# Attention plus top-2 experts on one core: experts read their weights in place, the bias comes from ScalarE, the dispatched rows are fp32

## The chip, the cores and the metric

The kernel is one launch on one NeuronCore of a Trainium2 chip. It is timed in device microseconds, as the median of several executions. Engines are named as in the profile: PE (TensorE, with PEld for its weight loads), DVE (VectorE), ACT (ScalarE), POOL (GpSimd) and SP (the queue that issues most transfers).

## The reference, cut to what matters

```python
xn = layernorm(x)                      # x is (2, 1024, 128)
# attention, causal, one head of 128
k, q, v = xn @ Wk.T + bk, xn @ Wq.T + bq, xn @ Wv.T + bv
attn = softmax(where(causal, q @ k.T * 128 ** -0.5, -inf)) @ v
# experts: 16, of which each token takes 2; hidden size 512
logits = xn @ Wr + br
topv, topi = top_k(softmax(logits), 2)
h = relu(xn @ W1[e] + b1[e])           # for both experts of the token
y = h @ W2[e] + b2[e]
out = x + attn + sum over the two experts of gate * y
```

There are 2048 tokens, so 16 tiles of 128 tokens, 16 experts, and 4096 pairs of token and expert.

## The kernel before

The program is written by hand for each engine; an engine runs its list in the order in which it stands, and semaphores join the lists. Five stages follow each other, with work of the next stage put into gaps of the one before.

1. **Front.** x comes in four groups of four tiles. DVE takes the moments (L641, L644), ACT the root (L498), DVE normalises into `xn` (L651). PE transposes (L903), ACT copies to `xT` (L503), PE multiplies with the router weights (L909). Before its first transpose of x, PE waits in its list for the loads of Wq, Wk, Wv, bq and bk (`proj_in`) and transposes the three matrices (L920).
2. **Routing.** When all logits are there, DVE chooses the two best experts of each token with compares and maxima over 128x256 (L703 to L719). PE counts ranks (L954 to L958) and DVE turns them into one slot number for each pair (L727 to L746). Between these, PE projects q, k and v (L942, L946) and ACT copies them out of PSUM (L534, L537).
3. **Dispatch and attention, tiles 0 to 12.** POOL scatters the normalised rows, 32 times 128 rows, into a table in DRAM of 47 tiles of 128 slots, sorted by expert (L467). A row is the fp16 high half, the fp16 low half, the number of the pair and the gate. The table was filled first with one blank row everywhere (L339). Beside this, PE, DVE and ACT do the attention: scores (L974), row maximum (L763), exponential (L558), transposes (L987), copies (L567, L773), product with v (L1005), sum into x (L783). Into this loop ACT's squares of the weights (L524) and fp16 high parts (L548), DVE's low parts (L755) and four of POOL's six high parts (L447) are put. Each expert's W1 and W2 are scaled by a power of two and kept as high and low fp16 halves; the fp32 weights come through a ring of six places (`raw`).
4. **Experts, 47 tiles.** Each tile belongs to one expert, whose number the engines read at run time. For each tile SP copies the expert's "kit" (W2 in two halves, a selector row, b2, a factor: 352 KB) from one place of SBUF to another (L351). PE transposes the slot rows (L1038, L1039), ACT copies them (L596), PE adds b1 with four matmuls against the selector (L1074) and multiplies with W1, three fp16 matmuls for each of four chunks (L1080, L1081, L1083). ACT takes the relu (L613), DVE the low half (L855), PE multiplies with W2, twelve matmuls (L1051 to L1053), DVE scales and adds b2 (L845), ACT multiplies with the gate (L602), POOL scatters the result rows by pair number (L478).
5. **Tail.** Attention of the three last tiles, then the two expert rows of each token are added to x by DVE (L871) and POOL (L487), and stored (L386).

PE runs two tiles deep: the W2 product of tile j-2 is laid between the chunks of tile j, and the transposes of tile j+2 follow. The address of each W1 chunk is worked out on PE's sequencer from the expert's number. The number is loaded once a tile:

```python
if c == 1 and j + 1 < TILES:
    after = expert_of(j + 1)        # one value_load a tile
if r is not None:
    if c == 1:
        result_waits(r); result(r, 0); result(r, 1)
    elif c > 1:
        last = result(r, c)
```

Of the kernel before, what the change touches and what calls it, by code (L numbers as in the profile page):

```python
# [11 lines left out]
I32 = mybir.dt.int32  # L12

P = 128
# [3 lines left out]
def attention_and_top2_experts(nc, x, Wk, bk, Wq, bq, Wv, bv, Wr, br, W1, b1, W2, b2, out):  # L18

# [12 lines left out]
    assert D == P and HID == NCH * P  # L36


    ROW = 2 * D + 4

    W1_HI, W1_LO, KIT_AT = 0, HID, 2 * HID
    W2_HI, W2_LO, SEL, B2F = 0, HID, 2 * HID, (2 * HID + P) // 2
    CF = B2F + D
    KIT = 2 * (CF + 1)
    EW = KIT_AT + KIT
    RAW = 6
    WG = 2
    NST, NHB, NYB = 7, 3, 6  # L50
    XG = [0, 6, 16, 32, TILES]
    WL = [*range(0, E - 1, 2), E - 1, E]
# [3 lines left out]
    LATE = 3  # L56

    slots_dram = nc.dram_tensor("slots_dram", (P * TILES, ROW // 2), I32).ap()
    pairs_dram = nc.dram_tensor("pairs_dram", (NT * P * K, D), F32).ap()

    with ExitStack() as ctx:
# [6 lines left out]

        xin = sb("xin", [P, NT, D], F32)
        xn = sb("xn", [P, NT, D], F32)  # L70
# [4 lines left out]
        wts = sb("wts", [P, E, EW], F16)  # L75
        raw = sb("raw", [P, RAW, 2, HID], F32)
        probsT0 = sb("probsT0", [P, 2, G * P], F32)
# [3 lines left out]
        b1rows = sb("b1rows", [P, HID], F32)  # L81

        b1parts = [sb(f"b1parts{n}", [P, HID], F16) for n in range(2)]
        mv = sb("mv", [P, NT, 2], F32)
        std = sb("std", [P, NT], F32)
        rstd = sb("rstd", [P, NT], F32)
        epsc = sb("epsc", [P, 1], F32)
        ident = sb("ident", [P, P], F32)
        ident16 = sb("ident16", [P, P], F16)

# [3 lines left out]
        scratch_i = sb("scratch_i", [P, 1], I32)  # L94
        past = sb("past", [P, E], F32)
        best = sb("best", [P, K, NT], F32)
        pick = sb("pick", [P, NT], F32)
        gap = sb("gap", [P, NT], F32)
        slotrow = sb("slotrow", [P, K, NT], I32)
        cnt = sb("cnt", [P, E], I32)  # L100
        ntile = sb("ntile", [P, E], I32)
        ntilef = sb("ntilef", [P, E], F32)
        cum = sb("cum", [P, E], F32)
        start = sb("start", [P, E], F32)
        expertf = sb("expertf", [P, 1], F32)
        expert = sb("expert", [P, 1], I32)
# [6 lines left out]
        b1s = sb("b1s", [P, 1], F32)  # L113
        b1tmp = sb("b1tmp", [P, E], F32)
        diag = sb("diag", [P, E], F32)
# [5 lines left out]

        slot_space = sb("slot_space", [P, TILES * ROW], F16)
        slots = slot_space[:, :].rearrange("p (t c) -> p t c", t=TILES)
# [9 lines left out]
        def early(n, parts=P):  # L133
            a = 2 * taken[0]
            taken[0] += n
            assert 2 * taken[0] <= stage_w + ybuf_w
            return space[0:parts, a:a + 2 * n].bitcast(F32)
# [1000 lines left out]
```

## Time and profile before

| | us |
|---|---|
| median of 3 executions | 242.03 |
| lowest, highest | 241.85, 243.75 |
| span of the profiled execution, first to last instruction | 237.6 |
| from the span to the median | 4.4 |

| stage | us from the span's start |
|---|---|
| first PE work on the loaded matrices | 8.5 |
| slot numbers of all pairs ready, first row maximum | 43.8, 43.9 |
| first matmul of the first expert tile | 111.9 |
| last W2 matmul of the last expert tile | 214.9 |
| end | 237.6 |

The profiled execution has no time of its own here beside its span. Busy time is 174.0 us on PE, 135.2 on DVE, 119.0 on ACT and 121.4 on POOL, so that no engine is busy throughout, and the stages have to be read one by one. In the page's slices PE is busy for a tenth or less from about 75 to 90 us, in the middle of the attention.

### The profile page before, as it was taken

What the parts mean: (1) busy time and instruction counts of PE and PEld (TensorE: products, weight loads), DVE (VectorE), ACT (ScalarE), POOL (GpSimd) and SP (SyncE); (2) the same over time, 40 slices, a digit from 0 to 9 for tenths busy, and PEclk for the clock granted to TensorE, in tenths of its full rate; (3) what the DMA queues carried; (4) which work ended last, traced back from release to release, by engine and by line L of the source; (5) the groups of instructions that cost most, each with busy time, mean ns of one, the idle gap of its engine ahead of it and who ended that gap; (6) DMA issues with size and microseconds to landing.
All of it is one profiled execution on the core that took longest, in us unless ns stands there. A gap on an engine that the chain in (4) does not pass through costs nothing.

```text
span 237.6 us, 5504 instructions
## 1 busy us (share of the span) xinstructions
PE 174.0 (73%) x1852; PEld 147.5 (62%) x1852; DVE 135.2 (57%) x318; ACT 119.0 (50%) x262; POOL 121.4 (51%) x146
## 2 busy tenths in 40 slices
PE   7549969759675002995989788988989879968940
PEld 7449645438474001874888777877878769855740
DVE  3893789798531004579768945444444543445491
ACT  1425496767541004496859546455464564544500
POOL 8593906388777770015049864534535445346250
PEclk9995597997958755599999999999999999999996
DMA  5879999419966110524995364653655554300682
GB/s 156 238 259 257 165 141 149 126 37 335 289 212 262 45 56 11 177 80 168 316 360 217 145 244 146 228 187 150 234 183 198 207 212 159 139 25 0 191 274 66
DMA packets 30202, 41.82 MB, mean 176 GB/s; under 512 B 5665, under 2 KB 18347, under 8 KB 29920
## 3 DMA queue, kind: packets, MB, share of 16 engines
q1 hardware_dynamic: 27648, 37.24, 52.6%
q0 software_dynamic: 2528, 4.24, 5.4%
q8 instruction: 16, 0.26, 0.5%
q14 instruction: 10, 0.08, 0.1%
HBM read 16.09 MB, written 9.39 MB: 107 GB/s over the span
## 4 chain that ended last, share of the span: by engine, by line
PE 37%; DVE 26%; another core or an unknown queue 17%; issue 10%; ACT 7%; DMA 1%; DVEq 0%; ACTq 0%
PE pO L1051 4%; DVE wts L755 4%; PE pS L1083 4%; DVE xn L651 4%; PE pS L1074 4%; PE pO L1005 4%; PE pS L974 3%; PE pS L1080 3%; PE pS L1081 3%; ACT xT L596 3%; PE pO L1053 2%; PE pO L1052 2%; PE pT L1039 2%; PE pT L987 2%
## 5 line engine op out<-in xcount | busy, mean ns | idle before, releaser
L478 POOL DMA_INDIRECT pairs_dram<-space,slot_space x47 | 48.8, 1038 | 56.4 <-ACT space L602 47.8
L855 DVE SCALAR_TENSOR_TENSOR xT<-pS,xT 128x512 f16<-128x512 f32 x47 | 32.5, 691 | 45.3 <-issue 22.9
L1051 PE MATMUL pO<-space,xT 128*128 128x128 f16 x188 | 38.5, 219 | 10.6 <-issue 6.0
L613 ACT ACTIVATE xT<-pS 128x512 f16<-128x512 f32 x47 | 27.9, 594 | 32.0 <-PE pS L1083 26.4
L467 POOL DMA_INDIRECT slots_dram<-slot_space,slotrow x32 | 34.6, 1080 | 14.8 <-issue 9.5
L1080 PE MATMUL pS<-xT,wts 128*128 128x128 f16 x188 | 38.8, 219 | 0.3 <-issue 0.3
L1083 PE MATMUL pS<-xT,wts 128*128 128x128 f16 x188 | 38.8, 219 | 0.0
L1081 PE MATMUL pS<-xT,wts 128*128 128x128 f16 x188 | 38.8, 219 | 0.0
L1052 PE MATMUL pO<-space,xT 128*128 128x128 f16 x188 | 38.5, 218 | 0.0
L1053 PE MATMUL pO<-space,xT 128*128 128x128 f16 x188 | 38.5, 218 | 0.0
L1051 PEld LDWEIGHTS pO<-space,xT 128*128 128x128 f16 x188 | 18.2, 97 | 15.0 <-issue 9.6
L987 PE MATMUL pT<-ident,xn 128*128 128x128 f32 x72 | 12.3, 302 | 20.3 <-ACT xn L558 20.2
L987 PEld LDWEIGHTS pT<-ident,xn 128*128 128x128 f32 x72 | 9.3, 156 | 24.3 <-ACT xn L558 23.6
L447 POOL TENSOR_TENSOR wts<-raw,wscale 128x1024 f16<-128x1024 f32 x6 | 11.4, 1906 | 23.7 <-DVE wscale L672 23.7
L755 DVE SCALAR_TENSOR_TENSOR wts<-raw,wscale,wts 128x1024 f16<-128x1024 f32 x16 | 23.2, 1450 | 0.2 <-ACT wts L548 0.2
L596 ACT COPY xT<-pT 128x256 f16<-128x256 f16 x47 | 17.4, 372 | 11.0 <-remote 7.6
L1074 PE MATMUL pS<-space,b1parts 128*128 128x128 f16 x188 | 18.6, 221 | 4.4 <-ACT xT L596 2.7
L1081 PEld LDWEIGHTS pS<-xT,wts 128*128 (+1 forms) x188 | 21.5, 115 | 0.5 <-issue 0.4
L1080 PEld LDWEIGHTS pS<-xT,wts 128*128 (+1 forms) x188 | 21.5, 114 | 0.3
L1083 PEld LDWEIGHTS pS<-xT,wts 128*128 (+1 forms) x188 | 21.5, 115 | 0.0
L974 PE MATMUL pS<-kT,qT 128*128 128x512 f32 (+3 forms) x48 | 20.1, 539 | 0.7 <-ACT v L537 0.7
L602 ACT ACTIVATE space<-space,slot_space 128x128 f32<-128x128 f32 x47 | 19.2, 411 | 2.3 <-DVE space L845 2.3
(144 smaller groups left out, 396.1 us busy)
## 6 DMA issues: line engine op xcount, KB each, us to landing
space<-wts SPq DMA_DIRECT2D x47, 352.5 KB
raw<-in_L_ffn_W SPq DMA_DIRECT2D x14, 512.0 KB, 5.3
slots_dram<-space SPq DMA_DIRECT2D x1, 3055.0 KB, 27.4
raw<-pairs_dram SPq DMA_DIRECT2D x8, 256.0 KB, 5.0
slot_space<-slots_dram SPq DMA_DIRECT2D x1, 1040.0 KB, 8.8
xin<-in_L_attn_x SPq DMA_DIRECT2D x4, 256.0 KB, 3.5
wts<-in_L_ffn_b SPq DMA_DIRECT2D x1, 1024.0 KB, 29.7
raw<-in_L_ffn_W SPq DMA_DIRECT2D x4, 256.0 KB, 2.9
```

The source lines that it names most:

```text
L467: pool.indirect_dma_start(slots_dram, bass.IndirectOffsetOnAxis(ap=slotrow[:, k, t:t + 1], axis=0), rows_i[:, k, t, :], None).then_inc(row ...
L478: pool.indirect_dma_start(pairs_dram, bass.IndirectOffsetOnAxis(ap=slots_i[:, j, D:D + 1], axis=0), ybuf[:, j % NYB, :], None, bounds_chec ...
L613: nc.scalar.activation(hid[:, j % NHB, 0, :], pA(j), ACT.Relu).then_inc(hi_done, 1)
L755: dve.scalar_tensor_tensor(out=low_part(e), in0=raw[:, e % RAW, :, :], scalar=wscale[:, e:e + 1], in1=high_part(e), op0=ALU.mult, op1=ALU. ...
L855: dve.scalar_tensor_tensor(out=hid[:, j % NHB, 1, :], in0=pA(j), scalar=0.0, in1=hid[:, j % NHB, 0, :], op0=ALU.max, op1=ALU.subtract).the ...
L1051: pe.matmul(y, h_hi, w_hi, start=(c == 0), stop=False)
L1052: pe.matmul(y, h_hi, w_lo, start=False, stop=False)
L1053: return pe.matmul(y, h_lo, w_hi, start=False, stop=(c == NCH - 1))
L1074: pe.matmul(bank[:, c * P:(c + 1) * P], b1parts[j >= B1_SECOND][:, c:HID:NCH], stage[:, j % NST, SEL:SEL + P], start=(c == 0), stop=False, ...
L1080: pe.matmul(to, w_hi, x_hi, start=False, stop=False, skip_group_check=True)
L1081: pe.matmul(to, w_hi, x_lo, start=False, stop=False, skip_group_check=True)
L1083: ins = pe.matmul(to, w_lo, x_hi, start=False, stop=(c == NCH - 1), skip_group_check=True)
```

## The change

- **Front.** ACT normalises (with a bias that DVE prepares), directly into fp32 rows of 128 values plus two numbers. DVE chooses the two best experts by `max` and `max_index`, one group of four tiles at a time, between the moments of later groups. The blank table is filled right after the loads of x, before the loads of Wq, Wk, Wv, bq and bk, in pieces of four rows (2,080 B) instead of one (520 B).
- **Weights.** `wts` has 18 places of 4 KB for each partition; the fp32 weights of expert e come into place e+2, all of them at once, and the fp16 halves are written into places e and e+2, in place. The ring, the kits and their copies, the selector and `b1rows` are gone. b2 stands in a table of its own. ACT makes all high parts, POOL none.
- **Attention.** Tiles 0 to 13 stand before the experts, 14 and 15 behind. The v bias is added by DVE when it copies v out of PSUM. The rank comes from a running sum of the choices and only the counts go through PE.
- **Experts.** ACT writes b1 of the tile's expert into the PSUM bank before the matmuls, which add to it. The slot rows are transposed once in fp32; ACT writes the high half, DVE the low half. The numbers of the experts are loaded in batches of twelve. W1 and W2 are both read from `wts` at an address worked out from the number. W1's twelve matmuls and W2's twelve stand one after the other. The gate isn't in the slot row: the final sum multiplies with it.
- **Tail.** DVE makes the final sum alone, 32 operations of 128x128, once all attention tiles are done.

Cut to its core:

```diff
-    ROW = 2 * D + 4
-    RAW = 6
-    NST, NHB, NYB = 7, 3, 6
-    XG = [0, 6, 16, 32, TILES]
-    LATE = 3
+    ROW = D + 2
+    NHB, NYB, NXS, NPB = 3, 6, 3, 4
+    XG = [0, 4, 12, 24, TILES]
+    IDS = 12
+    LATE = 2
+    NBL = 4
 # SP
             load_x(3)
+            sp.wait_ge(blank_made, 1)
+            sp.dma_start(blank_v[:, 0:whole, :].rearrange("p (m n) c -> p m (n c)", n=NBL),
+                         blank_i.rearrange("p n c -> p (n c)")[:, None, :].broadcast_to([P, TILES // NBL, NBL * ROW])
+                         ).then_inc(blank_sent, 16)
+            sp.dma_start(blank_v[:, whole:TILES, :], blank_i[:, 0:TILES - whole, :]).then_inc(blank_sent, 16)
             for n, w in enumerate((Wq, Wk, Wv)):
                 sp.dma_start(wqkv[:, n, :], w).then_inc(proj_in, 16)
...
-            sp.dma_start(slots_v, blank[:, None, :].broadcast_to([P, TILES, ROW // 2])).then_inc(blank_sent, 16)
...
+            for n in range(1, NW):
+                load_weights(n)
 # ACT
+            def normalise(g):
+                act.wait_ge(nbias_done, g + 1)
+                for t in range(G * g, G * g + G):
+                    ins = nc.scalar.activation(rows[:, t, 0:D], xin[:, t, :], ACT.Identity, bias=nbias[:, t:t + 1],
+                                               scale=rstd[:, t:t + 1])
+                ins.then_inc(xn_done, 1)
             for g in range(NG):
                 std_of(g)
+                normalise(g)
                 if g == 0:
                     act.wait_ge(wT_done, 1)
...
+            def put_bias(j):
+                load_ids(j)
+                ...
+                nc.scalar.copy(pA(j).rearrange("p (c s) -> p c s", s=P),
+                               b1s[:, bass.ds(ids[j], 1), :].rearrange("p a c -> p (a c)")[:, :, None].broadcast_to(
+                                   [P, NCH, P])).then_inc(bias_put, 1)
 # DVE
+            def choose(g):
+                dve.wait_ge(logits_done, g + 1)
+                ...
+                for t in tiles:
+                    ins = dve.max(top[:, t, :], lg[:, t, :])
+                step(ins)
+                for t in tiles:
+                    ins = dve.max_index(pick[:, t, :], top[:, t, :], lg[:, t, :])
+            moments(0)
+            moments(1)
+            inverse_std(0)
+            moments(2)
+            inverse_std(1)
+            dve.wait_ge(router_in, 32)
+            dve.wait_ge(consts, 1)
+            choose(0)
+            moments(3)
+            inverse_std(2)
+            choose(1)
+            inverse_std(3)
+            choose(2)
+            step(choose(3))
...
             def combine(n):
                 dve.wait_ge(pairs_in[n], 16)
                 for k in range(K):
-                    ins = dve.tensor_tensor(xin[:, here, :], xin[:, here, :], pairs[:, here, k, :], ALU.add)
+                    for t in range(TYL * n, TYL * n + TYL):
+                        ins = dve.scalar_tensor_tensor(out=xin[:, t, :], in0=pairs[:, t, k, :],
+                                                       scalar=gate[:, k, t:t + 1], in1=xin[:, t, :], op0=ALU.mult,
+                                                       op1=ALU.add)
 # PE
+            router(NG - 1)
+            for n in range(4):
+                project_qk(n)
+            pe.wait_ge(sofar_done, 1)
...
+            def hidden(j):
+                load_ids(j)
+                e = ids[j]
+                pe.wait_ge(bias_put, j + 1)
+                pe.wait_ge(xs_lo, j + 1)
+                pe.wait_ge(wlo_done, min(j, E - 1) + 1)
+                for c in range(NCH):
+                    w_hi = part(e, HI)[:, :, c:HID:NCH].rearrange("p a h -> p (a h)")
+                    w_lo = part(e, LO)[:, :, c:HID:NCH].rearrange("p a h -> p (a h)")
+                    pe.matmul(to, w_hi, x_hi, start=False, stop=False, skip_group_check=True)
+                    pe.matmul(to, w_hi, x_lo, start=False, stop=False, skip_group_check=True)
+                    ins = pe.matmul(to, w_lo, x_hi, start=False, stop=True, skip_group_check=True)
```

In the fences below, `ISA` is a register instruction of PE's sequencer that works out an address from the expert's number, and the rows are in the order of PE's list. One expert tile before, from the first W1 chunk of a tile in mid-stage to the third (L1080 to L1083 are W1, L1051 to L1053 are W2):

```order
L1080 ISA
L1080 MATMUL pS<-xT,wts 128x128
L1081 MATMUL pS<-xT,wts 128x128
L1083 ISA
L1083 MATMUL pS<-xT,wts 128x128
L1051 MATMUL pO<-space,xT 128x128
L1052 MATMUL pO<-space,xT 128x128
L1053 MATMUL pO<-space,xT 128x128
```

The same place now, at the change from W1 (L981 to L983) to W2 (L999 to L1001):

```order
L981 ISA
L981 MATMUL pS<-xT,wts 128x128
L982 MATMUL pS<-xT,wts 128x128
L983 ISA
L983 MATMUL pS<-xT,wts 128x128
L999 ISA [waits y_done,lo_done]
L999 MATMUL pO<-wts,xT 128x128
L1000 ISA
L1000 MATMUL pO<-wts,xT 128x128
L1001 MATMUL pO<-wts,xT 128x128
```

The W2 matmuls had none of these rows and now have two for each three matmuls, as W1 has: 16 a tile instead of 8.

SP's list before, from the last load of x:

```order
L309 DMA xin<-in_L_attn_x 128x4x128
L318 DMA space<-in_L_attn_Wq 128x128
L318 DMA space<-in_L_attn_Wk 128x128
L318 DMA space<-in_L_attn_Wv 128x128
L319 DMA bqk<-in_L_attn_bq 128x1
L320 DMA bqk<-in_L_attn_bk 128x1
```

And now:

```order
L287 DMA xin<-in_L_attn_x 128x4x128
L303 DMA slots_dram<-slots 128x11x520 [waits blank_made]
L306 DMA slots_dram<-slots 128x390
L308 DMA slots<-in_L_attn_Wq 128x128
L308 DMA slots<-in_L_attn_Wk 128x128
L308 DMA slots<-in_L_attn_Wv 128x128
L309 DMA bqk<-in_L_attn_bq 128x1
L310 DMA bqk<-in_L_attn_bk 128x1
```

The fill of the table, 3 MB, moved from behind three pairs of weight loads to ahead of the five loads that PE's first work waits for.

## Rows read from the trace of the kernel before

**Rows 1.** The page's first line, and what the DMA engines moved in 40 equal slices.
```profile
span 237.6 us, 5504 instructions
...
GB/s 156 238 259 257 165 141 149 126 37 335 289 212 262 45 56 11 177 80 168 316 360 217 145 244 146 228 187 150 234 183 198 207 212 159 139 25 0 191 274 66
```
**Rows 2.** The fill's transfer: count, KB each, median us from issue to landing.
```profile
slots_dram<-space SPq DMA_DIRECT2D x1, 3055.0 KB, 27.4
```
**Rows 3.** Order of time, front: start, us, engine, line, operation, count, [idle before <-releaser].
```profile
8.53 0.55 PE L920 MATMUL pO<-ident,space 128*128 128x128 f32 x3 [2.10 <-DMA bqk<-in_L_attn_bk]
19.16 1.73 PE L909 MATMUL pO<-wr,xT 128*128 128x16 f32 x8
20.73 1.09 PE L903 MATMUL pT<-ident,xn 128*128 128x128 f32 x4
24.89 3.76 PE L942 MATMUL pS<-xT,space 128*128 128x512 f32 x4
43.92 0.29 DVE L763 CUSTOM_DVE_ANT_0 pS<-pS,causal 128x128 f32<-128x128 f32 x1
```
**Rows 4.** Groups by line: count, busy us, mean ns | idle before, its releasers.
```profile
L602 ACT ACTIVATE space<-space,slot_space 128x128 f32<-128x128 f32 x47 | 19.2, 411 | 2.3 <-DVE space L845 2.3
L641 DVE BATCH_NORM_STATS2 space<-xin 128x6 f32<-128x128 f32 x16 | 3.4, 276 | 3.8 <-DMA xin<-in_L_attn_x 3.8
L534 ACT ACTIVATE kT<-pS,bqk 128x512 f32<-128x512 f32 x4 | 2.7, 687 | 2.0 <-PE pS L942 2.0
L524 ACT ACTIVATE wts<-raw 128x1024 f16<-128x1024 f32 x16 | 17.0, 1063 | 0.2 <-issue 0.2
L543 ACT ACT_TABLE_LOAD x1 | 1.3, 1283 | 0.0
L548 ACT ACTIVATE wts<-raw,wscale 128x1024 f16<-128x1024 f32 x10 | 11.5, 1150 | 5.6 <-DVE wscale L672 5.5 <-issue 0.2
L558 ACT ACTIVATE xn<-pS,negm 128x128 f32<-128x128 f32 (+7 forms) x16 | 12.0, 747 | 5.3 <-DVE negm L763 3.6 <-issue 1.6
L558 ACT ACTIVATION_READ_ACCUMULATOR xn<-pS,negm 128x1 f32 x16 | 3.2, 201 | 0.0
L567 ACT COPY probsT<-pT 128x512 f32<-128x512 f32 (+2 forms) x8 | 3.8, 479 | 5.1 <-remote 2.8 <-PE pT L987 2.3
```
**Rows 5.** Order of time around the idle stretch of the attention: POOL, PE, ACT.
```profile
44.88 1.18 POOL L467 DMA_INDIRECT slots_dram<-slot_space,slotrow  x1 [5.32 <-DVE slotrow L746]
72.73 1.61 PE L1005 MATMUL pO<-v,probsT 128*128 128x128 f32 x12
87.94 0.96 POOL L467 DMA_INDIRECT slots_dram<-slot_space,slotrow  x1 [0.30 <-issue]
92.55 0.59 ACT L567 COPY xT<-pT 128x512 f32<-128x512 f32 x1 [18.96 <-remote]
```
**Rows 6.** Busy time of the expert stage: stretch, length, engines, clock, DMA.
```profile
112.00:215.00 103.00, 88.65 (x1411) 81.21 (x1411) 55.96 (x110) 58.57 (x147) 49.51 (x46) 1.00 0.53 195
```
**Rows 7.** Order of time on PE, second expert tile, full clock.
```profile
113.38 0.22 PE L1080 MATMUL pS<-xT,wts 128*128 128x128 f16 x1
113.43 0.22 PE L1081 MATMUL pS<-xT,wts 128*128 128x128 f16 x1
...
113.68 0.24 PE L1080 MATMUL pS<-xT,wts 128*128 128x128 f16 x1
...
113.93 0.24 PE L1080 MATMUL pS<-xT,wts 128*128 128x128 f16 x1
```
**Rows 8.** Groups by line: the expert tile on ACT and DVE, the final sum.
```profile
L613 ACT ACTIVATE xT<-pS 128x512 f16<-128x512 f32 x47 | 27.9, 594 | 32.0 <-PE pS L1083 26.4 <-remote 4.8 <-issue 0.8
L855 DVE SCALAR_TENSOR_TENSOR xT<-pS,xT 128x512 f16<-128x512 f32 x47 | 32.5, 691 | 45.3 <-issue 22.9 <-ACT xT L613 22.2
L783 DVE SCALAR_TENSOR_TENSOR xin<-pO,rinv,xin 128x128 f32<-128x128 f32 x16 | 5.3, 337 | 2.1 <-issue 2.0
L871 DVE TENSOR_TENSOR xin<-xin,raw 128x256 f32<-128x256 f32 x10 | 5.9, 600 | 2.1 <-DMA raw<-pairs_dram 1.9
```

More of the change, by code:

```diff
@@ L12 @@
 I32 = mybir.dt.int32
+U32 = mybir.dt.uint32
 P = 128
@@ L413, in _ @@
-            step(pool.memset(ones[:, :], 1.0))
-            pool.affine_select(out=later[:, :], in_=later[:, :], compare_op=ALU.is_gt, fill=-1.0,
+            pool.memset(ones16[:, :], 1.0 / P)
+            step(pool.memset(before[:, :], 1.0))
+            pool.affine_select(out=before[:, :], in_=before[:, :], compare_op=ALU.is_gt, fill=0.0,
                                base=0, pattern=[[1, P]], channel_multiplier=-1)
-            for k in range(K):
-                pool.iota(rows_i[:, k, :, D:D + 1], pattern=[[K * P, NT], [0, 1]], base=k, channel_multiplier=K)
@@ new lines, in _, with scales @@
+            dve.wait_ge(ex_done, 1)
+            step(dve.tensor_reduce(exsum[:, :], ex[:, :, :], AX.X, ALU.add))
+            step(dve.reciprocal(gate[:, 0, :], exsum[:, :]))
+            dve.tensor_tensor(gate[:, 1, :], gate[:, 0, :], gap[:, :], ALU.mult).then_inc(gates_done, 1)
+            def scales(g, bank):
+                s = slice(WG * g, WG * g + WG)
+                dve.wait_ge(sums_done, g + 1)
+                step(dve.tensor_scalar(expo[:, s], bank[:, s].bitcast(I32), 1, None, ALU.logical_shift_right))
@@ new lines, in _, with load_ids @@
+            dve.wait_ge(cf_made, 1)
+            dve.tensor_copy(cf[:, :], pO[1][:, 0:TILE_COLS]).then_inc(cf_done, 1)
+            ids = {}
+            def load_ids(j):
+                if j % IDS == 0:
+                    z = min(j + IDS, TILES)
+                    _, got = nc.values_load_multi_w_load_instructions(
+                        erow[0:1, j:z], engines=[mybir.EngineType.DVE], min_val=0, max_val=E - 1,
+                        skip_runtime_bounds_check_because="the numbers of experts are clamped")
+                    ids.update(zip(range(j, z), got))
@@ new lines, in _ @@
+            pe.wait_ge(sofar_done, 1)
+            count = sofar[:, :, NT - 1]
+            pe.matmul(pO[0][:, 0:E], before[:, :], count, start=True, stop=True)
+            pe.matmul(pO[0][:, E:2 * E], ones16[:, :], count, start=True, stop=True).then_inc(ranks_done, 1)
+            for n in range(4, 2 * NG):
+                project_qk(n)
+            for g in range(NG):
+                project_v(g)
+                if g == 0:
+                    pe.wait_ge(consts, 2)
+                    pe.wait_ge(spread_done, 1)
+                    pe.matmul(pO[1][:, 0:TILE_COLS], ones[:, :], spread[:, :], start=True, stop=True).then_inc(erow_made, 1)
```

900 lines of the change are left out of this document (378 added, 522 removed).

## The prediction

> **What bounds the kernel now.** I read the page first for the span and the slices, then the order of time stage by stage, then the groups by line for durations. The profiled execution spans 237.6 us [rows 1]; the median of the runs is 242.03, so 4.4 us lie around the span, and I add them at the end.
>
> Four stages follow each other. The front ends with the first row maximum, at 43.9 [rows 3]. The attention and the weights last until the experts begin, 68.0 us later, at 111.9 (table of stages). In the middle of them is a hold: PE runs its product with v at 72.7, but ACT's next copy starts only at 92.55, after 19.0 us of idle time that no signal of this trace closes ("remote"); POOL's scatters run from 44.9 to 88.9, and the copy comes 3.6 us after the last [rows 5]. That the scatters delay PE's signals is my reading of this neighbourhood, not something that a row states. The experts take 103.0 us for 47 tiles, 2.19 each, with PE busy for 88.7 of them at full clock [rows 6]. The tail takes 22.6.
>
> No engine is full throughout, so each stage is costed apart, by the wait that ends last in it.
>
> **The front: later by 17.6 us.** PE's first three transposes start at 8.53, when the last of the five matrix loads is there [rows 3]. Now the fill stands ahead of these loads on the same queue. It moves 3.1 MB; before, behind other loads, it took 27.4 us [rows 2]. How long it takes in 2,080 B pieces no row shows. Bounds: at the fastest slice of the page, 360 GB/s, 8.7 us; at the old time 27.4. I take the slices of the front, about 258 GB/s [rows 1], which gives 12.1, since those slices move similar loads; PE then begins at 20.6 instead of 8.5.
>
> The Trainium skill, "SBUF — State Buffer", section "Summary: rules for kernel authors", says to reckon about 358 GB/s between HBM and SBUF. By that rule the fill would take 8.7 us and the sum would be 3.4 lower. The busiest slice of the trace, 360 GB/s, is at that figure, the slices of the front are well under it.
>
> From there it is one chain, because ACT waits for PE's transposed matrices in its list between the first and the second group's normalising:
> - matrices transposed 0.55, copied out 0.5, root 0.3, DVE's reciprocal and bias 0.5, four normalises at 0.411 (the same shape on ACT, [rows 4]) 1.6, transposes 1.1 and router 1.7 at the lower clock (1.09 and 1.73, [rows 3]): first logits at 26.9.
> - A round for each later group, as choice and bias stand in one list on DVE: choice 2.1, bias 0.4, normalise 1.6, copy 0.6, transposes 1.1, router 1.7 = 7.5. The choice of a group is eight small operations and eight of one tile; I take 2.1 from the small operations of the trace (about 0.15 to 0.3 each). The first round has the last group's moments in it too, four at 0.276 [rows 4] plus as much as one more, 1.3: 8.8. So logits 2 to 4 are complete at 35.7, 43.2 and 45. Two more choices: 47.4.
> - PE projects q and k of half the groups before the ranks, four groups of matmuls, 3.76 at the lower clock [rows 3]: ranks at about 49, slot numbers about 4 later, at 53.
> - ACT meanwhile: the last of eight copies of q and k (0.687, [rows 4]) about 53.7, four squares at 1.06 and their reads to 58.3, table load and exponentials 1.9 (load 1.28) to 60.2; DVE then makes the gates, 1.1, and starts the first row maximum at about 61.5 instead of 43.9: **+17.6**. If the fill is at its bounds, +14.2 or +32.9.
>
> What stands on DVE behind the slots (expert numbers 1.2, four v copies, b1 sums) fits before the gates and costs nothing, unless ACT is earlier than this; then up to 3 us of it show.
>
> **Attention and weights: shorter by 14 us.** POOL's six high parts, the ring and its waits are gone, all weights are loaded ahead. ACT has now the most work: 12 squares at 1.06 (12.7), 13 high parts at 1.15 (15.0), 14 exponentials at 0.747 and a read of 0.201 (13.3), and 14 copies at 0.479 (6.7) [rows 4]: 47.7. With a few per cent for handing over, 50.5, and 3.5 for the last weight half, bias and rows of the first tile, 54 against 68.0: **-14.0**. This counts the hold as gone. Of the 68.0 it was some 20; the new work on ACT gives back 6. The bounds: the whole hold comes back (rival B), or DVE and ACT overlap perfectly, -18.
>
> **Experts: longer by 5.8 us.** Removed: four b1 matmuls, which run at the pitch of 0.055 that three matmuls in a row show [rows 7], 0.2 a tile; the gate operation, 0.411 on ACT, hidden; the kits, off the path. Added: eight address instructions on PE's sequencer for each tile, as W2 is now addressed like W1, and a batch of numbers every twelve tiles instead of one each tile. A W1 group of three matmuls with two such instructions starts 0.25 after the one before it (113.68 to 113.93), though its matmuls need 0.17 [rows 7]. Before, each such group was followed by a W2 group without any, in whose time the sequencer caught up. Now eight groups in a row at 0.25 make 2.0, and the waits and two transposes 0.25: 2.25 a tile. 47 x 2.25 + 3 to fill and drain = 108.8 against 103.0: **+5.8**. ACT would need 0.6 for the bias, 0.594 for the relu and 0.3 for the rows, 1.5; DVE 0.691, 0.3 and 0.34, 1.35 [rows 8]: both fit beside it. Bounds: ACT's work with its waits, 1.75 (rival C); upwards 2.4, if the waits on three semaphores cost twice as much.
>
> **Tail: shorter by 0.6 us.** Two attention tiles instead of three, about 4 us less. The final sum is 32 operations of the kind that takes 0.337, about 10 us with little of POOL's help; before, ten of 0.600 on DVE and six on POOL [rows 8]: +4 on DVE, of which 0.6 fit under the loads. Bounds ±4.
>
> **Sum.** 237.6 + 17.6 - 14.0 + 5.8 - 0.6 = 246.4 span; with 4.4 around it, 250.8, so 251 against 242.03.
>
> **Rivals.**
> - **B, the hold comes back.** The scatters start now at about 54 and take 44 us again (32 at 1.27 and 0.96 to 1.38 each); until 97 they lie beside the attention, which starts at 61.5. For it: the late copies lie within 4 us of the last scatter [rows 5]. If PE's signals are late until some 3.6 us after the last scatter, the attention stands for 10 to 30 us: 261 to 281, about 270. Against it: no kit, no ring and larger pieces stand in the DMA queues now.
>  The Trainium skill, "SBUF — State Buffer", section "SBUF: two separate sides", has it that "A DMA cannot be slowed by a compute op, and vice versa". By that rule alone there would be no hold and B would fall out. The trace speaks against leaning on it: ACT's 19 us idle stand exactly beside POOL's scatters.
> - **C, faster than before: the addresses don't limit.** The queue that fed 113.38 to 113.49 at 0.055 shows that instructions can be ready ahead. If the sequencer works ahead during each tile's waits, the 26 matmuls need 1.45 and ACT or the hand-over sets about 1.75 a tile: 47 x 1.75 + 3 = 85.3, that is -17.7 instead of +5.8, so 251 - 23.5 = 227.5. It decides from about 2.05 a tile on: below it, the kernel is as fast as before or faster. Against it: in steady state nothing replenishes a queue that drains at 0.25 a group.
> - **D, the fill does not hold the loads back.** The fill writes DRAM and the five loads are small; if they land at about 8.5 to 10 all the same, the front is 11 shorter: 240, no change.
> - **Combinations** of B with C, about 246, and of C with D, about 217.
>
> **Chances.** A (251, within 245 to 258) 0.38; B 0.26; C 0.16; D 0.08; B with C 0.06; the rest 0.06. The forecast is A's, 251; its own range 245 to 258. The range to hold 8 in 10 reaches to C's 226 and into B, 274. Faster by over 1% (below 239.6): C, C with D and a third of D, 0.21. Within 1%, which is about what a measurement of this kernel can tell from no change (239.6 to 244.4): the rest of D and the edges, 0.08. Slower by over 1%: A, B and most of B with C, 0.71.
>
> **What would show each step.** PE's first work on the loaded matrices at about 20.6 (17 to 36); were it at 9, D holds. First logits near 27, rounds of 7 to 9. Slot numbers near 53, the first row maximum near 61.5. From there to the first W1 matmul 54 us without a stretch in which PE, DVE and ACT all stand; a stretch of over 5 us beside the scatters is B. ACT's relu in the experts every 2.25 us; under 2.05 is C. The last part after the experts 22 us. The prediction is wrong if the front's loss is off by more than half, or if the expert tile does not keep to the address instructions.

## The result, and the profile after

The changed kernel took 288.12 us (median of 4 runs, 285.85 to 290.4) where the kernel before took 241.94: a ratio of 1.185, interval 1.175 to 1.196. Ratios and intervals are formed from the fast executions alone, those within 1.5 per cent of the fastest of their kernel. The forecast, 251, missed it, and so did its range, 226 to 274.

In the later runs both kernels were faster: before about 210.5 (on four chips), the changed kernel 254.5 (on two of them); ratio 1.210, interval 1.204 to 1.216. The record does not say on which chip the first runs were. The two numbers of the first runs are to be compared with each other, and the later ones with each other. By stage, from one profiled execution of each, in us:

| stage | before, first runs | changed, first runs | before, later | changed, later |
|---|---|---|---|---|
| to the first row maximum | 43.9 | 60.3 | 43.5 | 60.1 |
| to the first W1 or b1 matmul | 68.0 | 86.5 | 52.7 | 55.2 |
| to the first relu | 1.1 | 1.5 | 1.9 | 1.2 |
| relu 1 to relu 47 (46 tiles) | 99.5 | 108.0 | 84.1 | 108.0 |
| to the end | 25.0 | 28.1 | 25.9 | 28.2 |
| span | 237.6 | 284.4 | 208.1 | 252.6 |

The front of the changed kernel, first runs, in order of time: start, duration, and in brackets the idle time before and what ended it.

```profile
20.10 0.90 PE L829 MATMUL pS<-ident,slots 128*128 128x128 f32 x3 [12.31 <-DMA bqk<-in_L_attn_bk]
32.54 1.73 PE L807 MATMUL pO<-wr,xT 128*128 128x16 f32 x8
39.67 3.43 PE L807 MATMUL pO<-wr,xT 128*128 128x16 f32 x16
60.26 0.29 DVE L664 CUSTOM_DVE_ANT_0 pS<-pS,causal 128x128 f32<-128x128 f32 x1
```

PE's first work on the matrices moved from 8.53 [rows 3] to 20.10; the router's rounds start 7 to 8 us apart behind it (the first, left out here, at 25.0), and the first row maximum is at 60.26 (61.5 forecast). The fill itself:

```profile
slots_dram<-slots SPq DMA_DIRECT2D x1, 2860.0 KB, 14.4
```

The attention, first runs, in order of time, PE, ACT and the last scatter:

```profile
61.32 1.21 PE L874 MATMUL pS<-kT,qT 128*128 128x384 f32 x2
...
72.78 0.42 PE L874 MATMUL pS<-kT,qT 128*128 128x128 f32 x1
...
84.59 0.48 ACT L457 COPY probsT<-pT 128x384 f32<-128x384 f32 x1 [13.44 <-remote]
...
86.72 2.54 PE L874 MATMUL pS<-kT,qT 128*128 128x512 f32 x4
...
92.11 0.96 POOL L375 DMA_INDIRECT slots_dram<-rows,slotrow  x1 [0.30 <-issue]
...
98.07 0.59 ACT L457 COPY probsT<-pT 128x512 f32<-128x512 f32 x1 [10.25 <-remote]
...
100.05 0.58 PE L860 MATMUL pO<-sumsq,ones 128*128 128x2 f32 x2 [10.79 <-DVE xin L683]
```

And two of its groups by line:

```profile
L457 ACT COPY probsT<-pT 128x512 f32<-128x512 f32 (+3 forms) x16 | 8.0, 499 | 33.4 <-remote 31.0 <-PE pT L889 2.4
...
L646 DVE TENSOR_SCALAR expo<-pO 128x2 int32<-128x2 int32 x8 | 1.3, 160 | 28.0 <-remote 22.4 <-PE pO L861 5.5
```

The hold of [rows 5] is there again, and longer: ACT waits 31.0 us in all for PE's transposes in waits that the profile puts down to nobody ("remote"), and things move again at 98, some 5 us after the last scatter's end at 93.1. The trace also records when each semaphore rises, and this shows what is late. The semaphore for which the copy at 84.59 waits rose at 84.57, 13.5 us after the transposes that raise it had ended; for the copy at 98.07 it was 11.1 us. In this trace 24 of PE's 222 recorded signals rose over 0.3 us after the end of their instruction, in that of the kernel before 71 of 211, while none of ACT's or DVE's was over 0.03 late. In the 16 later traces none of PE's was over 0.015 late. Ends of matmuls are modelled, so it stays unsaid whether the signal or the end of the matmul itself was late. The same stretch in a later run, same kernel:

```profile
60.29 0.96 POOL L375 DMA_INDIRECT slots_dram<-rows,slotrow  x1 [0.30 <-issue]
...
60.99 0.48 PE L889 MATMUL pT<-ident,probs 128*128 128x128 f32 x1 [2.29 <-ACT probs L448]
...
61.50 0.27 ACT L457 COPY probsT<-pT 128x128 f32<-128x128 f32 x1
61.55 0.96 POOL L375 DMA_INDIRECT slots_dram<-rows,slotrow  x1 [0.31 <-issue]
```

```profile
L457 ACT COPY probsT<-pT 128x512 f32<-128x512 f32 (+3 forms) x16 | 7.9, 496 | 3.5 <-PE pT L889 3.5
```

Here the copy starts 0.03 us after the transpose ends, with the scatters at the same pace beside it, and its group idles 3.5 us instead of 33.4.

In the experts, one tile of the changed kernel, PE in order of time (first runs):

```profile
190.40 0.24 PE L981 MATMUL pS<-xT,wts 128*128 128x128 f16 x1
190.48 0.22 PE L982 MATMUL pS<-xT,wts 128*128 128x128 f16 x1
190.53 0.23 PE L983 MATMUL pS<-xT,wts 128*128 128x128 f16 x1
190.65 0.24 PE L981 MATMUL pS<-xT,wts 128*128 128x128 f16 x1
...
191.57 0.23 PE L999 MATMUL pO<-wts,xT 128*128 x1
191.69 0.23 PE L1000 MATMUL pO<-wts,xT 128*128 x1
191.75 0.22 PE L1001 MATMUL pO<-wts,xT 128*128 x1
191.81 0.23 PE L999 MATMUL pO<-wts,xT 128*128 x1
```

Most groups of three start 0.25 after the one before, W1 and W2 alike, as the groups in [rows 7] did; in this tile it is 0.24 to 0.31, and 0.36 at the change from W1 to W2. Three matmuls need 0.17. Overlapping matmuls count as busy, so the busy time hides these gaps. The tail's final sum is one block of 32 operations:

```profile
272.64 9.49 DVE L773 SCALAR_TENSOR_TENSOR xin<-slots,gate,xin 128x128 f32<-128x128 f32 x32
```

### The profile page after: what moved, and what is told of

Read it like the earlier page. It is cut to its first block, busy times and chain, and to the rows that moved or that the text cites. A ratio compares the mean times of both kernels' runs of the same rounds, so it can differ in the third digit from the quotient of the medians.

```text
span 284.4 us, 5460 instructions
## 1 busy us (share of the span) xinstructions
PE 203.9 (72%) x1628; PEld 161.6 (57%) x1628; DVE 138.8 (49%) x462; ACT 134.3 (47%) x274; POOL 82.0 (29%) x102
## 4 chain that ended last, share of the span: by engine, by line
PE 60%; another core or an unknown queue 11%; DVE 10%; ACT 7%; issue 5%; SPq 4%; DMA 3%; DVEq 0%; ACTq 0%
PE pS L981 8%; PE pO L1000 8%; PE pO L999 7%; PE pS L983 5%; PE pS L874 5%; PE pO L909 4%; PE pS L982 4%; PE pO L1001 4%; PE pS L815 3%; DVE xin L773 3%; PE pT L889 3%; DMA bqk<-in_L_attn_bk 3%; PE pT L966 2%; PE pO L807 2%
## 5 line engine op out<-in xcount | busy, mean ns | idle before, releaser
L382 POOL DMA_INDIRECT pairs_dram<-ybuf,pair x47 | 46.8, 996 | 122.4 <-DVE ybuf L743 116.4
L981 PE MATMUL pS<-xT,wts 128*128 128x128 f16 x188 | 46.8, 249 | 5.1 <-DVE xT L735 3.7
L375 POOL DMA_INDIRECT slots_dram<-rows,slotrow x32 | 31.0, 967 | 56.7 <-DVE slotrow L608 47.2
L983 PE MATMUL pS<-xT,wts 128*128 128x128 f16 x188 | 44.6, 238 | 0.0
L1000 PE MATMUL pO<-wts,xT 128*128 x188 | 42.9, 229 | 0.1
L999 PE MATMUL pO<-wts,xT 128*128 x188 | 42.9, 229 | 0.0
L982 PE MATMUL pS<-xT,wts 128*128 128x128 f16 x188 | 42.4, 226 | 0.0
L1001 PE MATMUL pO<-wts,xT 128*128 x188 | 41.4, 221 | 0.0
L511 ACT ACTIVATE xT<-pS 128x512 f16<-128x512 f32 x47 | 28.1, 597 | 16.2 <-PE pS L983 15.7
L493 ACT COPY pS<-b1s 128x512 f32 x47 | 27.8, 594 | 7.3 <-PE pS L938 4.8
L981 PEld LDWEIGHTS pS<-xT,wts 128*128 x188 | 21.6, 115 | 10.8 <-issue 6.1
L501 ACT CAST xT<-pT 128x128 f16<-128x128 f32 x47 | 12.4, 266 | 28.2 <-PE pT L966 26.6
L889 PE MATMUL pT<-ident,probs 128*128 128x128 f32 x72 | 13.5, 325 | 16.9 <-ACT probs L448 6.9
L982 PEld LDWEIGHTS pS<-xT,wts 128*128 x188 | 25.0, 133 | 0.1
L457 ACT COPY probsT<-pT 128x512 f32<-128x512 f32 (+3 forms) x16 | 8.0, 499 | 33.4 <-remote 31.0
L999 PEld LDWEIGHTS pO<-wts,xT 128*128 128x128 f16 x188 | 18.2, 97 | 7.9
L909 PE MATMUL pO<-v,probsT 128*128 128x128 f32 x144 | 21.9, 306 | 0.0
L983 PEld LDWEIGHTS pS<-xT,wts 128*128 x188 | 21.6, 115 | 0.4
L909 PEld LDWEIGHTS pO<-v,probsT 128*128 128x128 f32 x144 | 20.6, 220 | 1.7 <-issue 1.3
L1000 PEld LDWEIGHTS pO<-wts,xT 128*128 128x128 f16 x188 | 18.1, 96 | 5.9 <-issue 0.2
## 6 DMA issues: line engine op xcount, KB each, us to landing
slots_dram<-slots SPq DMA_DIRECT2D x1, 2860.0 KB, 14.4
```

The lines of the kernel that those rows point to most:

```text
L375: pool.indirect_dma_start(slots_dram, bass.IndirectOffsetOnAxis(ap=slotrow[:, k, t:t + 1], axis=0), rows_i[:, t, :], None).then_inc(rows_s ...
L382: pool.indirect_dma_start(pairs_dram, bass.IndirectOffsetOnAxis(ap=pair[:, j:j + 1], axis=0), ybuf[:, j % NYB, :], None, bounds_check=NT * ...
L511: nc.scalar.activation(hid[:, j % NHB, 0, :], pA(j), ACT.Relu).then_inc(hi_done, 1)
L909: ins = pe.matmul(pO[t % 2][:, 0:D], probsT[t % 2][:, j // G, j % G * P:(j % G + 1) * P], v[:, t // TB * TB + j, :], start=(j == 0), stop= ...
L981: pe.matmul(to, w_hi, x_hi, start=False, stop=False, skip_group_check=True)
L982: pe.matmul(to, w_hi, x_lo, start=False, stop=False, skip_group_check=True)
```

## The experiments

In all of them the kernel before ran beside on the same chip and took 209.7 to 210.5 us.

**1. The fill behind the five loads.** Edit, in SP's list of the changed kernel:

```diff
-            sp.wait_ge(blank_made, 1)
-            sp.dma_start(blank_v[:, 0:whole, :]...)
             for n, w in enumerate((Wq, Wk, Wv)):
                 sp.dma_start(wqkv[:, n, :], w).then_inc(proj_in, 16)
...
+            sp.wait_ge(blank_made, 1)
+            sp.dma_start(blank_v[:, 0:whole, :]...)
```

> The changed kernel with the fill of the slot table moved behind the loads of Wq, Wk, Wv, bq and bk; nothing else. Theory: the 11.6 us by which PE's first work on the matrices came later (20.1 against 8.5) are the fill's, and the front is one chain behind it: PE's three transposes at about 9, slot numbers about 41 instead of 52.2, first row maximum about 49 instead of 60.3. The stretch in which PE's signals come late is tied to the scatters and moves with them, so the total is about 11 us shorter, 275 to 279. Rival: the chain behind is set by other loads (the weights for the squares, the fill for the scatters), and less than 5 us are gained.

Measured: 240.74, span 239.0 against 252.6, so 13.6 less than in a later run of the unchanged kernel.

```profile
8.17 0.55 PE L829 MATMUL pS<-ident,slots 128*128 128x128 f32 x3
...
47.53 0.29 DVE L664 CUSTOM_DVE_ANT_0 pS<-pS,causal 128x128 f32<-128x128 f32 x1
```

PE begins at 8.17 and the first row maximum is at 47.53 instead of 60.09. The expectation had the gain about right (11); its total of 275 to 279 was that of the first runs, with their hold. So 12.6 of the 16.6 us of the front are the fill's place in SP's list. The other 4.0 stay with the new routing and normalising; they were not taken apart.

**2. Two scatters under way at most.**

```diff
+                    pool.wait_ge(rows_sent[i % 2], 16 * (i // 2))
                     pool.indirect_dma_start(slots_dram, ...).then_inc(rows_sent[i % 2], 16)
```

> The changed kernel, but each of the 32 row scatters first waits until the scatter two before it has landed, so that two are under way at most; same work. Theory: PE's signals come late because scatters follow each other every 1.27 us without a pause and their writes pile up; spread to 2 us or more each, the signals are prompt (under 0.5 us), the stretch of 61.6 to 98 is gone, the attention takes about 52 us (60 to 112), and the total falls by 20 to 35 us, to 253 to 268. Rival 1: any scatter beside PE delays it, as many as there are: the delay lasts as long as the scatters do, now longer, and the total is the same or more. Rival 2: the idle stretch is PE's low clock and has nothing to do with POOL: nothing changes.

Measured: 254.64, and 255.22 on another chip. Neither showed late signals, with or without the edit (the unchanged kernel: 254.5), so this tells nothing about them. Nor did the edit pace much: the scatters take 54.5 to 99.5 instead of 52.5 to 95.6, but the usual distance of two of them is 1.27 to 1.28 us, where it is 1.26 without the edit. Even where signals are late it would not have been a clean test of the pace.

**3. The scatters after the attention.**

```diff
                 for t in range(NT):
+                    if k == 0 and t == 2:
+                        pool.wait_ge(o_read, NT - LATE)
```

> The changed kernel, but 30 of the 32 row scatters wait until the attention of tiles 0 to 13 is over. Theory (scatters delay PE's signals): the attention runs without the idle stretch, 60 to about 113, then 30 scatters stand alone, 38 us, and the experts begin at about 113 + 38 + 11 = 162; total about 300. It tells how long the attention is by itself. Rival (the stretch has another cause, the clock or the loads): the attention still takes about 80 us, the experts begin at 190, total near 325.

Measured: 292.37. From the first row maximum to ACT's first bias copy the attention takes 50.9 us (62.1 to 113.0) without scatters, and 52.7 (60.1 to 112.8) with them in a later run of the unchanged kernel; in the other later traces of this attention with scatters it takes 51.2 (experiment 2) to 53.2. So without late signals the scatters cost it 0.3 to 2.3 us in all. Total and stage are near the expectation, but since the unchanged kernel has no hold there either, the two theories were not told apart.

**4. Plain writes of the same rows.** As 3, with this in SP's list:

```diff
+            for i in range(K * NT):
+                sp.dma_start(spare[P * i:P * i + P, :], rows_i[:, i % NT, :]).then_inc(spare_sent, 16)
```

> As the run before (30 of 32 scatters after the attention), and in the time of the scatters SP issues 32 plain transfers of the same rows, 128 pieces of 520 bytes each, to a spare table in DRAM. Theory A: it is POOL's own issuing of descriptors that delays PE: no idle stretch here, attention about 53 us. Theory B: it is the traffic of small writes: the idle stretch is back, attention 70 us or more.

Measured: 291.75, no hold; the attention takes 50.9, as in 3. Inconclusive for the same reason. SP issued the transfers from 54.6 to 68.9, so they lay beside the first part of the attention alone.

**5. Both kernels again, unchanged.**

> The kernel before, unchanged. In the last runs it took 210.5 us beside the experiments, against 241.9 in the runs shown first, and the profile of one experiment showed prompt PE signals beside scatters that follow each other every 1.27 us. Theory: the stretch in which PE's signals come late belongs to the chip or its condition, not to the program: where the total is 210 the stretch 62.5 to 92.5 is gone and the experts are shorter too; where it is 242 it is there. Rival: the two totals differ by something else, such as the clock or the expert stage alone, and the stretch is there in both.

> The changed kernel, unchanged, several rounds beside the kernel before on one chip. Theory: without the late signals, before is 210.5 and the changed kernel 288 less its own stretch (36 us), 250 to 254; the ratio is then near 1.20, made by the front (16 us), the longer expert tile and the handing over. With the late signals, 242 and 288 as before. Rival: the late signals cost both kernels the same, and the difference stays 46 us.

> The changed kernel, unchanged, beside these. 288 where the kernel before takes 242, 254 where it takes 210; a third pairing (288 beside 210, or 254 beside 242) would show that the late signals do not belong to the chip but come and go by the execution.

Measured: before 209.96; changed 254.54 (4 runs; 253.34 to 255.03) and, on a further chip, 254.47. The totals 242 and 288 were seen in the first runs alone, in all 4 executions of each kernel; 210 and 254.5 in all later ones. The same groups of copies in the kernel before, first runs and then a later one:

```profile
L567 ACT COPY xT<-pT 128x512 f32<-128x512 f32 (+1 forms) x8 | 4.2, 528 | 22.1 <-remote 19.0 <-PE pT L987 3.1
L773 DVE COPY xT<-pT 128x256 f32<-128x256 f32 (+1 forms) x4 | 2.2, 555 | 20.5 <-remote 19.9 <-issue 0.6
...
L567 ACT COPY xT<-pT 128x512 f32<-128x512 f32 (+1 forms) x8 | 4.2, 525 | 2.7 <-PE pT L987 2.7
L773 DVE COPY xT<-pT 128x256 f32<-128x256 f32 (+1 forms) x4 | 2.2, 550 | 2.8 <-PE pT L987 2.8
```

So the hold was in the profile from which the forecast was made. By these differences late signals cost the kernel before 15.3 us in the attention (68.0 against 52.7) and as many in the experts (99.5 against 84.1), and the changed kernel 31.3 in the attention and none in the experts.

Why the experts differ can be read from the traces of the first runs. In the kernel before 61 of 134 PE signals of that stage are over 0.3 us late (2.2 at most), and 59 of the 61 lie beside two scatters of result rows that POOL issued back to back; there are 22 such pairs. In the changed kernel there are 6 pairs, and all of its 12 late signals lie beside them. Scatters in pairs are not enough for it, though: the later traces have 4 and 5 pairs and no late signal. The difference of the two kernels is nearly the same with late signals (46.2) and without (44.0), by chance of these sums.

**6. W2 at a fixed place.** Every tile multiplies with expert 0's W2; the result is that of other weights, the work is the same.

```diff
             def result(r):
-                e = ids[r]
+                e = 0
```

> The changed kernel, but the W2 product of every tile reads expert 0's halves at a fixed place: 8 address instructions a tile on PE's sequencer instead of 16, all matmuls kept (the result of the experts is thereby not the reference's). Theory: the tile of 2.35 us is set by the address instructions; 8 fewer at 0.125 give at least 0.5 us back, after which ACT's and DVE's hand-over sets it, 1.75 to 1.85 a tile; relu 1 to relu 47 takes 80 to 86 us instead of 108, total 227 to 232 beside a kernel before of 210. Rival: ACT's three operations and waits, or the order of the matmuls, set the tile: no change, 252 to 255.

Measured: 220.7, 33.8 less than 254.5; 1.65 us a tile on average, 1.51 in the median tile.

**7. W1 fixed as well.** The same edit in `hidden`.

> As the run before, and W1 fixed at expert 0 too: no address instruction for PE is left in the expert tile (the result of the experts is thereby not the reference's). Theory: if the run with W2 fixed was already set by ACT and DVE, this gives little more, 1.7 to 1.85 a tile; if the address instructions still set it, 26 matmuls at 0.055 and the waits remain, 1.5 to 1.6.

Measured: 215.87, 1.55 a tile on average, 1.46 in the median tile. PE's matmuls now start 0.05 to 0.06 apart:

```profile
149.99 0.22 PE L981 MATMUL pS<-xT,wts 128*128 128x128 f16 x1
150.05 0.22 PE L982 MATMUL pS<-xT,wts 128*128 128x128 f16 x1
150.11 0.22 PE L983 MATMUL pS<-xT,wts 128*128 128x128 f16 x1
150.16 0.22 PE L981 MATMUL pS<-xT,wts 128*128 128x128 f16 x1
```

With 16, 8 and 0 address instructions the median tile takes 2.29, 1.51 and 1.46 in the later runs. The first eight cost nearly nothing, the second eight 0.8. The reading that fits all three is that the sequencer has room for eight beside the matmuls and then becomes the bound, at 0.1 for each instruction.

**8. The kernel before, W2 read in place.**

```diff
-                w_hi, w_lo = s[:, W2_HI + c * P:W2_HI + (c + 1) * P], s[:, W2_LO + c * P:W2_LO + (c + 1) * P]
+                w_hi = wts[:, bass.ds(expert_in[r], 1), at_hi:at_hi + P].rearrange("p a h -> p (a h)")
+                w_lo = wts[:, bass.ds(expert_in[r], 1), at_lo:at_lo + P].rearrange("p a h -> p (a h)")
```

> The kernel before with one part of the change: the W2 matmuls read the halves from the resident weights at an address worked out from the expert's number, not from the kit (which is still copied, since it brings b2 and the selector). PE's list keeps its order, W1 and W2 groups in turn. Theory: the eight added address instructions alone make the tile long, from 1.83 to about 2.4 (16 at 0.125, four b1 matmuls 0.22, two transposes and a number's load), total 210 + 46 x 0.5 = 233 to 240. Rival (the order of W1 and W2 in two blocks is what costs): under 1.95 a tile, total below 216.

Measured: 251.91, 2.76 a tile instead of 1.83. This one part of the change costs the kernel before 41.4 us, more than expected; the changed kernel's tile is 0.4 shorter than this one. It has no b1 matmuls, loads its numbers twelve at a time and has one transpose; which of these makes the 0.4 was not tested.

**9. W1 and W2 groups in turn,** in the changed kernel, as in the kernel before (result(r, c) behind each chunk of `hidden`).

> The changed kernel with W1 and W2 groups laid in turn as before, the same 16 address instructions. Theory (the instructions count, not their order): 2.25 to 2.35 a tile, total 252 to 255; the single tiles of 2.8 to 3.0 us, where PE waited at the border of the two blocks, may go, so at best 5 us are gained. Rival (order): 1.85 a tile, total near 231.

Measured: 256.21, 2.37 a tile. The order is not the cause.

**10. W2 copied again, fill behind.** `result` reads a ring of four, and SP gets the old job back:

```diff
+                for a, at in enumerate((2 * HID, 2 * WSLOT)):
+                    w = flat_i[:, at // 2:at // 2 + E * WSLOT // 2].rearrange("p (e c) -> p e c", c=WSLOT // 2)
+                    sp.dma_start(stage_i[:, j % NST, a, :], w[:, bass.ds(e, 1), HID // 2:HID]...)
```

> The changed kernel with two parts undone: the fill behind the five loads (240.7 by itself), and W2 read at fixed places again, from a ring of four kits of 256 KB that SP copies out of the resident weights by the expert's number (into the buffer of the attention's probabilities, idle in that time). PE has 8 address instructions a tile, as with W2 fixed. Theory: 1.65 to 1.75 a tile, so 240.7 less 30 to 34, 207 to 211, as fast as the kernel before on the same chip (210.5) or up to 3 us faster. Rival: the copies (47 kits in 78 us, 154 GB/s) come late through a ring of four, or PE waits for them; then over 1.9 a tile and a total above 218.

Measured: 221.73 (4 runs), ratio to before 1.051 (1.046 to 1.056). The median tile is 1.51, but the mean 1.95: single tiles of 8.3, 3.9 and 5.5 us. In the first of them lies one wait for a kit that stood behind 1.5 MB of slot rows in the queue; the other two were not traced to a cause:

```profile
119.01 0.27 PE L1023 MATMUL pO<-probs,xT 128*128 128x128 f16 x1 [4.92 <-DMA probs<-wts]
```

**11. Slot rows first, a ring of eight, the tail shared.**

```diff
-    NST = 4
+    NST = 8
+            for n in POOL_SUMS:
```

> The run before (fill behind the five loads, W2 copied by SP) with four things mended: all slot rows are fetched before the first kit, so that kits no longer queue behind 1.5 MB (the 8.3 us gap between two tiles); a ring of eight kits instead of four; the gates are made behind the first two row maxima; in the tail ACT scales and POOL adds three of the eight parts of the final sum. Theory: the long gaps of 8.3, 3.9 and 5.5 us between tiles go, 1.65 a tile as with W2 fixed (-12 to -14 us), the front is 1.2 shorter and the tail 2 to 3: 204 to 209, so 1 to 3 per cent faster than the kernel before where that takes 210.5. Rival: the copies themselves are the limit, not the queue; the tile stays at 1.9 and the total at 215 to 219.

ACT scales and POOL adds parts 1, 4 and 6 of the final sum.

Measured: 212.06 (6 runs) against 209.71; ratio 1.012 (1.005 to 1.018). 1.75 a tile, with one of 4.9 left, in which PE waits 1.9 for a kit. DVE's 20 remaining operations of the sum took 7.85 us, against 9.49 for 32 without POOL: sharing gave 1.6 us, not the 3.6 of twelve operations. DVE in the stretch beside POOL's last four adds (200.76 to 203.84), and behind them, where the number after the length is its busy time and the count of its operations stands in brackets (one counts in both):

```profile
200.70:203.90 3.20, 3.17 (x5) 1.00 0.01 2
203.90:208.50 4.60, 4.39 (x16) 0.54 0.56 161
```

Four of DVE's operations run beside the adds. They take 0.76 to 0.88 each, about as long as one add (0.72 to 0.76), and the other sixteen 0.34 to 0.35. So beside the adds DVE gets through one operation in the time of one add, and these four lose the 2 us that are missing.

**12. The border of attention and experts.**

```diff
-                ins = pe.matmul(pA(n), ident[:, :], xT[:, 0:512], start=True, stop=True)
+                w0 = high_part(0)[:, 0, :]
+                ins = pe.matmul(pA(n), w0[:, 0:P], w0, start=True, stop=True)
```

> The run before (ring of eight kits) with the handing over from the attention to the experts shortened: the four matmuls that only set up the PSUM banks use fp16 halves of a weight instead of fp32 (3.6 us on PE before the first bias copy, about 0.9 expected), ACT copies the first tile's slot rows before the biases of tiles 1 and 2 (1.1 us), and POOL makes the high parts of experts 13 to 15, ACT none of them among the first tiles. Theory: first relu at about 99.3 instead of 103.1, the first eight tiles 1 to 2 us shorter: 206 to 208 against 209.7, 0.5 to 1.5 per cent faster. Rival: the wait is shifted to DVE's scale factor and slot rows (cf at 99.3) and less than 1.5 us is gained: 210 to 212, not faster than the kernel before.

Measured: 210.04 (12 runs) against 210.38, ratio 0.999 (0.994 to 1.003). The tiles became shorter (1.68), the first relu came only 0.8 earlier: PE waited 3.1 us for DVE's spread of the scale factors. The fence shows one of the four edits that the expectation lists.

**13. Transposes ahead of that wait.**

```diff
+            slot_transpose(0)
+            slot_transpose(1)
             pe.wait_ge(o_read, NT - LATE)
             pe.wait_ge(factor_done, 1)
             pe.matmul(pO[1][:, 0:TILE_COLS], ones[:, :], spread[:, :], ...)
-            slot_transpose(0)
-            slot_transpose(1)
```

> The run before (e11_mended), with PE's two transposes of the first slot rows laid ahead of the matmul that spreads the scale factors, since PE waited 3.1 us for DVE's spread there and the transposes stood behind it. Theory: ACT's copies of the slot rows fall into that wait, the first relu comes at about 101 instead of 102.3, and the total is 208.5 to 209.5, 0.5 per cent below the kernel before. Rival: DVE's list (factor, copy, slot rows) ends last anyway and nothing is gained: 210, the same as the kernel before.

Measured: 208.89 (6 runs, 205.6 to 210.42) against 209.85 (208.95 to 210.99), by the medians 0.5 per cent less. The ratio 0.985 (0.978 to 0.992) rests on the three shortest of the six runs, so it is not shown that this version beats the kernel before; it beats the changed kernel by far, through the edits of 10 to 13 together. The first relu comes 0.2 earlier than in 12, not 1.3, and the first row maximum, ahead of the edit, came 1.0 earlier in that execution, so no gain of the edit itself is seen. PE, in order of time:

```profile
95.58 1.03 PE L998 MATMUL pS<-wts 128*128 128x512 f16 x4
96.45 0.38 PE L1023 MATMUL pT<-ident,slots 128*128 128x128 f32 x2
99.48 0.39 PE L1063 MATMUL pO<-spread,ones 128*128 128x48 f32 x2 [2.66 <-DVE spread L770]
100.93 0.24 PE L1038 MATMUL pS<-xT,wts 128*128 128x128 f16 x1 [1.05 <-DVE xT L794]
```

**Pacing once more**, on the chip of 12:

> The changed kernel with two row scatters under way at most, once more. If the kernel before takes 242 on this chip (late PE signals): the pacing theory says 250 to 262 with prompt signals, the rival 285 or more. If the kernel before takes 210, nothing is told about the late signals: 253 to 256, as before.

It is the 255.22 of experiment 2.

## Why the prediction was wrong, step by step

- **Front: right.** +17.6 forecast, +16.3 measured. PE's first work was put at 20.6 and came at 20.10, so that the fill put it off by 11.6, where 12.1 was forecast. Rival D is refuted, and experiment 1 shows the place in the list as the cause.
- **Attention: the step that failed.** It said -14.0, "This counts the hold as gone". The new work was sized well: 54 forecast, 55.2 measured where there is no hold. But 54 was set against a 68.0 that contained one, of 15.3 us by the later runs and not "some 20", and nothing in the change was shown to remove it. In the first runs the changed kernel took 86.5, +18.5, with 31.0 us of ACT's waits for late PE signals. Like with like, the stage is 2.5 longer. Of the miss of 37 us in the first runs, 32.5 are here.
- **Rival B was the case, but too small.** It named the place and the sign in the trace, and gave 10 to 30 us on top of A, 261 to 281. The hold was 31.3 by the difference of first and later runs (86.5 against 55.2), just over B's upper end; the rest up to 288 is mostly what experts and tail had been given too little. In the kernel before, the attention had run from 43.9 to 62.5, while the scatters came at up to 2.3 us distance, before it stood; here the scatters had been 1.27 apart since 54, before the attention began, and it stood almost from its first tile. I put it at 0.26 against 0.38, on the argument that the DMA queues were emptier. Nothing in the trace said that queues were its cause.
- **Experts: the mechanism right, the term too small.** 2.25 a tile forecast, 2.30 in the median tile, 2.35 on average; +5.8 forecast, +8.5 in the first runs, +23.9 in the later ones. The address instructions are the bound (6, 7, 8), the order is not (9), and C is refuted. The 2.19 of the kernel before were not its own pace either: 1.83 without late signals. The changed kernel's tile is the same in first and later runs (108.0 in both): of its PE signals in this stage only 12 of 130 were over 0.3 late, 1.1 at most, and that PE is the bound in it may hide these (not tested).
- **Tail: wrong by 3.7 us.** -0.6 forecast, +3.1 measured in the first runs. In the later traces the part behind the last relu takes 26.5 to 28.2 with the same tail, against 25.9 before, so +0.6 to +2.3. The 10 us of the sum were right (9.49), but they start only when the attention has ended, with nothing laid under the loads.
- **The two rules cited.** The Trainium skill's rule of "SBUF — State Buffer", section "SBUF: two separate sides", spoke against B. The later runs come near to it: scatters cost the attention 0.3 to 2.3 us. In the first runs the hold beside the scatters was there in both kernels. The runs do not say whether it has to do with SBUF at all. The Trainium skill's 358 GB/s, from the same page's section "Summary: rules for kernel authors", gave 8.7 us for the fill; measured were 14.4 from issue to landing, and 11.6 for its 3.1 MB from the landing of the last x load (7.4) to 19.0, an estimated 270 GB/s. The trace agrees with that figure neither here nor where the fp32 weights come in, at 406 and 412 GB/s in the two fastest slices.
- **The 4.4 us around the span** were too many. The changed kernel's profiled execution took 286.11 with a span of 284.4, so 1.7 lie around it; the 4.4 were the difference of a span and a median over several executions.

**What stays open:** what makes PE's signals late in the first runs. They lie beside scatters 1.27 us apart in both kernels, in the attention as in the experts; DVE's and ACT's signals were prompt; and the hold ends 3.6 and 5 us after the last scatter. That the scatters cause it is not shown: pace, place and traffic of the scatters were to tell the causes apart and fell on runs without late signals. Nor is it shown that it belongs to a chip; a condition that had passed by the later runs would look the same. The granted clock, 0.74 in the hold's attention and 0.90 in the later one, goes with PE's idling and cannot make a copy start 13.5 us after its transposes' end.

## What to carry to other kernels

A stage in which every engine stands, and whose waits the profile puts down to nobody, is not a property of the kernel until it has been seen in runs at another time and on another chip; forecast with it on both sides or on neither, and never let a change "remove" it without an edit that touches its cause. Count the address instructions that a queue must issue beside its matmuls: here eight a tile were nearly free, and from there on each cost its full tenth of a microsecond. And in a list of transfers, what the first compute waits for stands first; 3 MB ahead of 200 KB cost 12.6 us at the first row maximum and 13.6 of the span.

## What the runs showed of the hardware

- PE's median expert tile took 1.46, 1.51 and 2.29 us with 0, 8 and 16 address instructions and the same 25 matmuls and transposes.
- The same program at the same pace of scatters ran with prompt PE signals (none over 0.015 us late) and with late ones (up to 18.8 us): 254.5 and 288 us; the kernel before 210.5 and 242. ACT's and DVE's signals were prompt in all of these.
- An operation of DVE with two SBUF inputs, 128x128 fp32, took 0.35 us alone, one started every 0.30, and 0.76 to 0.88 beside POOL's adds on 128x256.
- A kit of 256 KB behind 1.5 MB in the same queue made PE wait 4.92 us.
